# The first loads of a scan issued in the stage before, a second chunk mixed by VectorE, and a last store in four

## The reference

```python
# first layer, on the normalized x
xz = xn @ W_in.T;  x_ssm, z = xz[..., :Di], xz[..., Di:]
x_ssm = silu(conv4(x_ssm) + conv_b)
xp = x_ssm @ W_xproj.T;  B, C = xp[..., 1:17], xp[..., 17:]
dt = softplus(xp @ W_dt.T + b_dt) + 0.001;  A = -exp(A_log)
h = clip(exp(A * dt) * h + (1 - exp(A * dt)) / (A + 1e-8) * B * x_ssm, -10, 10)   # token by token
y = (sum_n C * h + D_param * x_ssm) * silu(z)
x = x + y @ W_out.T
# second layer, on the normalized x
w = sum of the two best softmax weights, divided by themselves
x = x + xn @ W_shared.T + w * (xn @ W_expert.T) + bias
```

## Time and profile before

| | us |
|---|---|
| runs | 4360.01 (median), 4350.95, 4363.68 |
| profiled execution, its time | 4355.76 |
| its span | 4353.9 |
| mean granted TensorE clock | 0.984 |
| TensorE, VectorE, ScalarE, GpSimd busy | 4164.5, 3663.8, 3174.8, 3102.1 |
| first DMA issue of the scan | 1022.16 |
| first DMA issue of `ffn` | 3469.04 |

### The profile page before, as it was taken

How to read it: one execution, slowest core, us unless ns; L and a number is a source line. 1 busy time by engine, 2 the same in 40 slices (tenths; PEclk the granted TensorE clock), 3 DMA queues, 4 the chain that set the end, 5 groups by cost and what they waited for, 6 DMA issues and landing times. The chain is left out here.

```text
span 4353.9 us, 48879 instructions
## 1 busy us (share of the span) xinstructions
PE 4164.5 (96%) x14186; PEld 2462.8 (57%) x14186; DVE 3663.8 (84%) x4288; ACT 3174.8 (73%) x5825; POOL 3102.1 (71%) x1546
## 2 busy tenths in 40 slices
PE   8999999995999999999999999999999869999999
PEld 6777777772444444444444444444444348888887
DVE  7888888884999999999999999999999854444443
ACT  5666666665999999999999999999999712111111
POOL 1110111002999999999999999999999857777772
PEclk9999999997999999999999999999999979999999
DMA  5777776657566657666765666576566365555550
GB/s 174 220 221 206 225 234 222 205 183 216 159 183 187 182 156 195 187 166 167 194 188 155 185 185 181 157 195 185 161 177 184 111 221 174 160 179 181 173 168 30
DMA packets 617005, 787.32 MB, mean 181 GB/s; under 512 B 116748, under 2 KB 344220, under 8 KB 616224
## 3 DMA queue, kind: packets, MB, share of 16 engines
q1 hardware_dynamic: 608288, 767.41, 60.8%
q10 hardware_dynamic: 8448, 16.78, 1.0%
HBM read 541.14 MB, written 244.85 MB: 181 GB/s over the span
## 5 line engine op out<-in xcount | busy, mean ns | idle before, releaser
L985 POOL TENSOR_TENSOR q<-g,cc 128x1024 f32<-128x1024 f32 x1024 | 2395.8, 2374 | 129.7 <-DVE g L1124 122.6
L1124 DVE TENSOR_TENSOR_SCAN g<-dd,carry,ps_a 128x512 f32<-128x512 f32 x2048 | 2400.3, 1256 | 32.7 <-ACT ps_a L1007 28.1
L1064 PE MATMUL ps_y<-q,w_s 128*128 128x512 f32 x4096 | 2102.0, 594 | 10.3 <-DMA w_s<-w_d 5.4
L1007 ACT ACTIVATE ps_a<-dt_s,small 128x512 f32<-128x512 f32 x2048 | 1502.0, 733 | 5.4 <-DVE g L1124 5.4
L996 ACT ACTIVATE dd<-ps_d 128x512 f32<-128x512 f32 x2048 | 1288.3, 629 | 65.6 <-PE ps_d L1051 42.8
L1051 PE MATMUL ps_d<-dm,xk 99*128 99x512 f32 x2048 | 1129.4, 552 | 64.1 <-DMA dm<-band_d 26.3
L1051 PEld LDWEIGHTS ps_d<-dm,xk 99*128 99x128 f32 x2048 | 384.1, 188 | 1210.7 <-ACT dd L996 944.6
L1064 PEld LDWEIGHTS ps_y<-q,w_s 128*128 128x128 f32 x4096 | 773.5, 191 | 189.8 <-issue 56.5
L334 POOL TENSOR_TENSOR xnt_lo<-xnt_f,xnt_hi 128x512 fp32r<-128x512 f32 x62 | 81.0, 1307 | 580.2 <-ACT xnt_hi L371 580.2
L504 PE MATMUL ps_r_f<-xnt_hi,w_hi 128*128 128x512 f32 x1024 | 420.0, 410 | 3.8 <-DVE w_lo L687 3.8
L504 PE MATMUL ps_r_f<-xnt_lo,w_hi 128*128 128x512 f32 x1024 | 402.3, 393 | 0.0
(11 more groups left out here) (166 smaller groups left out, 4422.4 us busy)
## 6 DMA issues: line engine op xcount, KB each, us to landing
w_s<-w_d SPq DMA_DIRECT2D x256, 512.0 KB, 3.7
xk<-xt_d SPq DMA_DIRECT2D x768, 132.0 KB
xt_d<-xt_f SPq DMA_DIRECT2D x256, 256.0 KB, 3.0
cc<-c_d SPq DMA_DIRECT2D x128, 512.0 KB, 11.4
dm<-band_d SPq DMA_DIRECT2D x192, 264.0 KB
xs_d<-xs_f SPq DMA_DIRECT2D x128, 256.0 KB, 2.5
zs_d<-zs_f SPq DMA_DIRECT2D x128, 256.0 KB, 3.0
dt_d<-lg_f SPq DMA_DIRECT2D x32, 1024.0 KB, 6.7
```

The costliest lines, as they stand in the source:

```text
L985: pool.tensor_tensor(q[:, s % QB:s % QB + 2, :], g[:, s % GB:s % GB + 2, :], rows, ALU.mult).then_inc(s_q, 2)
L1007: act.activation(ps_a[:, s % AB, :], dt[:, blk % DTB, :], ACT.Exp, scale=small[:, blk % MD, S_A + n:S_A + n + 1]).then_inc(s_a, 1)
L1064: pe.matmul(ps_y[:, blk % 2, :], w[:, half % WB, at:at + P], q[:, s % QB, :], start=(n == 0), stop=(n == NS - 1)).then_inc(s_n, 1)
L1124: dve.tensor_tensor_scan(g[:, s % GB, :], dd[:, m % 2, n, :], ps_a[:, s % AB, :], carry[:, m, n:n + 1], ALU.add, ALU.mult).then_inc(s_g, 1)
```

## The change

1. `dm` and `xk` are now allocated before the front. The front uses their memory itself, for `xnt_hi`, `xnt_lo`, the last quarter of `w_lo` and for `w_dt`. Once it needs them no more, it issues the scan's first loads: pieces 0 and 1 of `dm` in the last chunk, after its fourth `xs` store, and after the last matmul of the projections pieces 2 and 3 and three halves of `xk`. `w`, `dt`, `cc` and some small tiles of the scan lie at other addresses.
2. The last `store_dt` is issued after these loads and the gathers, and the front no longer waits for it. VectorE waits for it at the scan's start. The flag `clips` is made before the last `add_positive`.
3. The scan's opening order on SyncE is shorter, and `w_s`, `b_ahead` and `x_prev` come sooner in it.
4. In `ffn`, y of chunk 1 is made by VectorE (`mixed`), piece by piece between the residuals of chunk 0 and later steps; ScalarE and VectorE split it in pairs, the first two pairs ahead of the normalization of chunk 0, the others behind it. TensorE has one `weigh` in place of two after each half projection of chunk 0, projects the first half of all four groups of chunk 1 first, and the second halves after the gates.
5. The last chunk's output is stored in four DMAs of 128 tokens.

```diff
+        with ExitStack() as both:
+            sb("fill_b", [P, 5 * NS], c=both)
+            dm = sb("dm", [P, NBLK, BLK, NS], F32R, both)
+            xk = sb("xk", [P, XB, NBLK // 2, P], F32R, both)
+            s_dm = [sem(f"s_dm{i}", both) for i in range(PIECES)]
+            s_xk = [sem(f"s_xk{i}", both) for i in range(XB)]
+            s_dto = sem("f_dto", both)
...
+def take_x(sp, xk, s_xk, xt_d, blk, h):
+    b, k, m = blk // MD // NCH, blk // MD % NCH, blk % MD
+    slot = (2 * blk + h) % XB
+    t0 = k * CH + (CH // 2) * h
+    for r, part in enumerate((0, 0, 1)):
+        src = xt_d[part, b, bass.ds(t0, BLK + 1), bass.ts(m, P)]
+        sp.dma_start(xk[(BLK + 1) * r:(BLK + 1) * (r + 1), slot, :, :].bitcast(F32),
+                     bass.AP(tensor=src.tensor, offset=src.offset,
+                             ap=[(DI, BLK + 1), (BLK * DI, NBLK // 2), (1, P)])).then_inc(s_xk[slot], 16)
+def take_b(sp, dm, s_dm, band_d, ch, i):
+    each = NBLK // PIECES
+    for r, part in enumerate((0, 1, 0)):
+        src = band_d[ch % 2, part, bass.ds(BLK * each * i, BLK + 1), NS:2 * NS]
+        sp.dma_start(dm[(BLK + 1) * r:(BLK + 1) * (r + 1), each * i:each * i + each, :, :]
+                     .rearrange("p g t n -> p g (t n)").bitcast(F32),
+                     bass.AP(tensor=src.tensor, offset=src.offset,
+                             ap=[(BAND - NS, BLK + 1), (BLK * BAND, each), (1, BLK * NS)])).then_inc(s_dm[i], 16)
...
+        w_dt = xk[0:NX3, 2, :, :].rearrange("p g c -> p (g c)")
+        w_lows = [w_lo[:, k, :] for k in range(KD - 1)] + [xk[:, 0:2, :, :].rearrange("p s g c -> p (s g c)")]
+        halves = dm[:, :, :, :].rearrange("p g t n -> p (g t n)").rearrange("p (e h q t) -> p e h q t", e=2, h=2, q=KD)
+        xnt_hi, xnt_lo = halves[:, :, 0, :, :], halves[:, :, 1, :, :]
...
+                    if ch == CHUNKS - 1:
+                        sp.wait_ge(s_diag, 16 * (4 + MD + 2))
+                        sp.wait_ge(s_mm, ch * PER)
+                        for i in range(2):
+                            take_b(sp, dm, s_dm, band_d, 0, i)
...
-                for h in range(2):
-                    store_dt(CHUNKS - 1, h)
+                sp.wait_ge(s_mm, CHUNKS * PER)
+                for i in range(2, PIECES):
+                    take_b(sp, dm, s_dm, band_d, 0, i)
+                for half in range(XB):
+                    take_x(sp, xk, s_xk, xt_d, half // 2, half % 2)
                 sp.wait_ge(s_xpo, CHUNKS * 32)
                 for b in range(BATCH):
                     gather_ahead(b)
+                for h in range(2):
+                    store_dt(CHUNKS - 1, h)
                 sp.wait_ge(s_diag, 16 * (4 + MD + 2 + BATCH))
-                sp.wait_ge(s_dto, CHUNKS * 32)
...
-                for h in range(2):
-                    add_positive(CHUNKS - 1, h)
                 dve.tensor_reduce(inside1[:, :], within[:, :, :], AX.XY, ALU.min).then_inc(s_fl, 1)
                 dve.wait_ge(s_fl, 2)
                 dve.tensor_scalar(clips[:, :], ps_xp[0:1, 0:1], P - 0.5, None, ALU.is_lt).then_inc(s_fl, 1)
                 dve.wait_ge(s_fl, 3)
-
-
-def scan(nc, sb, sem, clips, small, xs_d, dt_d, xt_d, bt_d, band_d, c_d, w_d, y_d, ba_d):
+                for h in range(2):
+                    add_positive(CHUNKS - 1, h)
...
-                load_x(0, 0)
-                load_b(0, 0)
-                load_b(0, 1)
-                load_x(0, 1)
-                load_b(0, 2)
-                load_b(0, 3)
                 load_dt(0)
-                load_dt(1)
                 load_c(0, 0)
                 load_c(0, 1)
-                load_x(1, 0)
+                load_w(0, 0)
+                load_ahead(0)
+                load_prev(0)
+                load_c(0, 2)
+                load_dt(1)
                 sp.wait_ge(s_dps, HALF)
                 load_x(1, 1)
-                load_w(0, 0)
+                load_c(0, 3)
                 load_w(0, 1)
-                load_c(0, 2)
-                load_c(0, 3)
-                load_ahead(0)
-                load_prev(0)
...
                 must_clip = dve.value_load(clips[0:1, 0:1], min_val=0, max_val=1)
+                dve.wait_ge(s_dto, CHUNKS * 32)
...
-                mix(1)
                 inverse_spread(0)
-                rest_of_y(1)
...
+                def upper_pair(ch, j):
+                    act.wait_ge(s_mul, piece(ch, 2 * j + 2))
+                    if ch > 0:
+                        act.wait_ge(s_o, SUB)
                     act.activation(y_hi[:, 2 * j:2 * j + 2, :], y[:, 2 * j:2 * j + 2, :], ACT.Copy).then_inc(s_yh, 1)
...
-                upper_y(1)
+                upper_pair(1, 0)
+                upper_pair(1, 1)
                 act.wait_ge(s_lo, len(parts))
                 normalize(0)
+                upper_turn(0, 0)
+                upper_turn(0, 1)
+                upper_pair(1, 2)
+                upper_turn(0, 2)
+                upper_turn(0, 3)
+                upper_pair(1, 3)
...
-                store(CHUNKS - 1)
-                for e in range(2):
-                    act.wait_ge(s_out[e], 16 * CHUNKS // 2)
+                last = CHUNKS - 1
+                for i in range(SUB):
+                    act.wait_ge(s_fin, last * SUB + i + 1)
+                    act.dma_start(out[bass.ds(last * CH + i * P, P), :], o[:, last % 2, i, :]).then_inc(s_out[last % 2], 16)
+                act.wait_ge(s_out[0], 16 * CHUNKS // 2)
+                act.wait_ge(s_out[1], 16 * (CHUNKS // 2 - 1 + SUB))
...
+                for i in range(SUB):
+                    project(0, i, 1)
+                    weigh(1, i)
+                weigh(1, 4)
+                pe.wait_ge(s_lo, len(parts))
+                turn(0, 0)
+                turn(0, 1)
+                weigh(1, 5)
+                project(1, 0, 0)
+                weigh(1, 6)
+                project(1, 1, 0)
+                turn(0, 2)
+                turn(0, 3)
+                weigh(1, 7)
+                project(1, 2, 0)
+                project(1, 3, 0)
+                gates_of(0)
+                weigh(2, 0)
+                project(1, 0, 1)
+                weigh(2, 1)
+                weigh(2, 2)
+                project(1, 1, 1)
+                weigh(2, 3)
+                weigh(2, 4)
+                project(1, 2, 1)
+                turn_gates(0)
+                weigh(2, 5)
+                weigh(2, 6)
+                project(1, 3, 1)
+                weigh(2, 7)
...
+                def finish_y(ch, m, z_m):
+                    dve.wait_ge(s_tt, piece(ch, m) + 1)
+                    dve.tensor_tensor(y[:, m, :], y[:, m, :], xs[:, m % XRING, :], ALU.add).then_inc(s_add, 1)
+                    dve.wait_ge(s_add, piece(ch, m) + 1)
+                    dve.tensor_tensor(y[:, m, :], y[:, m, :], z_m, ALU.mult).then_inc(s_mul, 1)
+                def mixed(m):
+                    self_term(1, m)
+                    dve.wait_ge(s_y[m // 2], 16 + 48)
+                    dve.wait_ge(s_zsl[m % ZRING], 16 * (m // ZRING + 1))
+                    finish_y(1, m, zs[:, m % ZRING, :])
...
-                for i in range(SUB):
+                for i in range(SUB - 1):
                     residual(0, i)
-                    self_term(1, 2 * i)
-                    self_term(1, 2 * i + 1)
+                    mixed(i)
+                lower_pair(1, 0)
+                residual(0, SUB - 1)
                 spread(0)
+                mixed(3)
+                shifted(0)
+                mixed(4)
+                lower_pair(1, 1)
+                mixed(5)
+                lower_turn(0, 0)
+                lower_turn(0, 1)
+                mixed(6)
+                lower_pair(1, 2)
+                mixed(7)
+                lower_turn(0, 2)
+                lower_turn(0, 3)
+                lower_pair(1, 3)
```

184 lines of the change are left out of this document (86 added, 98 removed).

## The result

The changed kernel takes 4321.75 us (median of 5 runs, 4320.37 to 4333.32), the kernel before 4358.97 in the same comparison (median of 5): a ratio of 0.9926, 95% interval 0.9913 to 0.9939, so 32 us less by the ratio, with 27 to 38 in the interval. The whole interval lies beyond the 0.3% under which the forecast spoke of no change. The forecast was 4322 us with a range of 4309 to 4337. The median lies on it, but the largest of the three terms of the sum does not: seam 1 gave 16 us and not 23, as the distances in the traces show.

The account below looks back on a forecast made before the run. GpSimd's 1024 multiplications set the scan's pace, and TensorE is always busy late in the last stage. Gains 23 + 11 + 2 = 36 us from 4355.8 give 4320, as a median 4322; range 4309 to 4337.

Parts of the forecast that it names:

- seam 1: From front to scan: GpSimd's fifth multiplication starts at 1049.5 in place of 1072.5, gain 23 us, bounds 16 and 26.
- the first rival: At the scan's start the queue stays the wall: gain 15 us, time 4328 to 4330; chance 0.16.
- the queue's bill at the barrier: Before the scan: moved loads take 25.4 us of queue, ending about 1021; scan begins about 1022.5, bound -3 to +2.
- a sign of being wrong: At the scan's start: SyncE's first issue of the scan later than 1025 would show the forecast wrong.
- The behaviour in the ring: At the front's end: one queue's descriptors go in ring order, so `ba_d` waits behind the moved loads; otherwise barrier 3 us earlier.
- From the barrier on: Scan's block 0: `ps_d` to last copy 12.3 us, first scan 2.1 later, multiplication 2.6 later; fifth's wait under 2 us.
- Pieces 0 and 1 cost the front nothing: Front's last chunk: their 9.1 us of loads delay no `zs` store; cost 0, bounds 0 and +1.5 us.
- Seam 2: Start of the last stage, to chunk 1's turn: normalization 12 us earlier, 1 lost; gain 11 us, bounds 5 and 13.
- The rival that it gives its gain back: Last stage: GpSimd's chunk 2 work ends 7 us late or short waits slow TensorE; 4 us left, 4329; chance 0.14.
- The end: Program's last output: three quarters of the store go earlier, gain 2 us, bounds 1 and 2.6.
- The slower rival: Scan: new addresses of `w`, `dt`, `cc` lengthen multiplications, 2422 ns each in place of 2374, time 4369; chance 0.02.
- The rival on the wall of the queue: Scan's start: multiplications 2 to 5 each wait 2 us for `cc`, losing 8; gain 15, 4328 to 4330; chance 0.16.

Follow-up runs that it names:

- The second comparison of the same kernels: The changed kernel, unchanged, timed again beside the kernel before: 4329.8 against 4359.1 us, ratio 0.9934.
- the four kernels: The changed kernel (profiled twice), it with the old `ffn`, and it with one last store: 4321.8, 4329.8, 4344.1 and 4329.0 us.
- rows_direct: The changed kernel with 14 small stores from SBUF in place of the two `ba_d` gathers: 4323.3 us, ratio 0.9919.
- the three old ones: The kernel before, it with the new `ffn` and one last store, and it with ScalarE's `upper_y(1)` moved later: 4359.0, 4346.5 and 4359.3 us.
- after: The changed kernel itself, in its first profile, against the kernel before: 4321.8 us, ratio 0.9926.
- pieces_late: The changed kernel with pieces 0 and 1 of `dm` issued with the other loads at the front's end: 4337.4 us, ratio 0.9960.
- direct_all: The changed kernel with small stores for gathers, five `cc` loads earlier, VectorE's `dt` wait inside its branch: 4320.0 us, ratio 0.9915.

## Right and wrong, step by step

- **The time, 4322 against 4321.75.** The agreement is partly luck. The second comparison of the same kernels gave 29.4 us in place of 37.2, and the measured parts add up to 30.3, not 36. By the base of the forecast (4355.8, and up to 4.3 for the median) 30.3 would have given 4325.5 to 4329.8, near the number of the first rival.
- **Seam 1, 23 us: wrong in size, 16.0.** The step that failed is the queue's bill at the barrier: "So the scan does not begin earlier: about 1022.5, as before", with a bound of +2. From the front's end it begins 4.2 us later (98.3 against 94.2 from G, the means of four and three); laid on the clock of the old trace that is 1026.6, beyond the 1025 that the forecast named as a sign of being wrong. The bill had the moved loads at 25.4 us and the gathers at nothing. The loads were not dearer than billed: they were over at G + 89.0, where the forecast had 1021, which is G + 92.7. What was missing is the gathers: SyncE waited 8.0 to 10.0 us for them in the four kernels, although their packets had run by G + 89.5, and without them (rows_direct) the barrier opens at G + 88.3. The `dt` stores behind them moved at 135 GB/s, where the forecast had 384, and `cc` comes behind all of it. From the forecast's 121.2 for the fifth multiplication (1049.5 from G) to the measured 127.5, the mean of four, it is 6.3 us: about 4.2 from the late barrier and 2.4 from the fifth's mean wait for `cc`. The rest of the gap from 23 is the old trace itself, whose fifth stood at 144.2, 1.4 us above the mean of the three old ones. That the fifth multiplication seemed to match within 3.3 us (1052.8 for 1049.5), and the first scan to come 15.1 us earlier as forecast (12.6 from G), is again the 2.5 us of the early front.
- **The behaviour in the ring: right, and of little weight.** The gathers' packets do run where the loads end: between 1013.9 and 1014.8 in after, and 7 us later, with the loads, in pieces_late. The Trainium skill (DMA: Bandwidth & Descriptors, section Queues, rings and completion order) says that an engine takes one queue's descriptors in ring order; these packets agree. But of the 8.0 us that SyncE waited, this order explains next to nothing, since SyncE's wait began about when the packets were over (1015.2). What the ring order was used for, to leave the barrier where it was, lacked the time from the gathers' packets to their completion.
- **From the barrier on: right.** First `ps_d` to last copy 12.4 us (forecast 12.3), first scan 2.1 behind it, first multiplication 2.6 behind that. The stall of the fifth was 1.2 to 3.7 us in four profiles, where under 2 was expected, so this part was a little low: each of them is a wait for `cc`.
- **Pieces 0 and 1 cost the front nothing: right.** No wait for a `zs` store, 59.4 us as before.
- **Seam 2, 11 us: right**, 12.2 by the distances, 9.5 in the pair of profiles first compared. From turn to turn 63.25 in place of 61 plus or minus 2, at the edge: the products `ps_b` wait 2.01 and 1.93 us for VectorE, and the matmuls behind each take 0.63 us for a while in place of 0.39. From chunk 1 on the turns are 50.45 us apart, as forecast. The rival that it gives its gain back had 7 us more in mind.
- **The end, 2 us: right**, 2.1.
- **The slower rival: fell.** A multiplication takes 2371 ns, before 2374.
- **The rival on the wall of the queue (0.16): this is what happened at seam 1**, in size (15 us forecast, 16.0 found) and partly in kind: `cc` did come last, but not four waits of 2 us each, rather a barrier 4 us late and one wait.

## What to carry to other kernels

Before loads are moved into a gap, list everything that already stands in that gap's queue with its time there and not by its bytes: a transfer of 1 KB in elements of 4 bytes held this queue as long as 1.7 MB of ordinary loads (8 us at 215 GB/s). An idle stretch ahead of a barrier in the old trace need not be slack: look which transfer the barrier waits for there. Count distances from the last common row that both traces share and not from the start of the span, since the same code reached that row anywhere within 6 us. And when a median agrees with a sum, look whether its terms do.

## What was not expected of the hardware

- Two gathers of 128 elements of 4 bytes each, DRAM to DRAM, were over in 0.4 to 1.3 us by their packets, but for the 8 us behind them the 16 DMA engines moved 21 to 30 GB/s at a share of 0.53 to 0.54, at two places of the program. In the old trace nothing at all is recorded from 1018 to 1022 while SyncE still waited, first for the `dt` stores and then 1.8 us for the gathers. Fourteen stores of 16 elements from SBUF cost the front nothing that shows (59.40 us).
- A queue with work in it holds the issuing engine too: nine `xk` loads took SyncE 8.5 to 9.5 us to issue behind 6 loads of `dm`, 13.5 behind 12 of them (pieces_late), 15.0 behind the gathers and 6, and 1.2 for three of them at an empty queue.
- After the wait for the `dt` stores VectorE shows nothing for 6.9 to 8.0 us until the branch's first instruction. With the wait put inside the branch (direct_all), that time passes before ScalarE is ready.
- The granted clock of TensorE fell to its lower level (1.2 GHz) for some us in one execution and not in another, behind short waits of the same length (a mean of 0.76 in the 5 us from 815, 0.68 in those from 4290), and each cost 1.4 to 1.6 us.
